# Loading and starting a recurrent kernel: biases spread by TensorE, the first x products split around the first gates, weights in halves, last outputs in pieces

## The chip, the cores and the metric

The kernel runs on one core of a Trainium2 chip. The metric is device time in microseconds for one execution, the median of several runs. TensorE (PE) multiplies into PSUM, VectorE (DVE), ScalarE (ACT) and GpSimd (POOL) do the rest, and the queues of SyncE (SP) and, after the change, of ScalarE issue the transfers, which 16 DMA engines carry out.

## The reference

A gated recurrent unit over 512 steps, batch 16, 512 channels, all in float32, with the input added to its output:

```
for each step t (H starts as cond_1024):
    Z = sigmoid(x_t Wxz' + bxz + H Whz' + bhz)
    R = sigmoid(x_t Wxr' + bxr + H Whr' + bhr)
    Ht = tanh(x_t Wxh' + bxh + (R * H) Whh' + bhh)
    H = Z * H + (1 - Z) * Ht
    out_t = x_t + H Whq' + bhq
```

## The kernel before, in words

**Layout.** A product has as its stationary operand a block of x or of the state (channels by 16 or 32 columns) and streams 64 to 192 columns of weights, so a gate's result lies in PSUM as four row groups of 32 (`j` in 0..3) by columns. VectorE turns it back (`turn_pre`, a 32x32 transpose) so that ScalarE can apply sigmoid or tanh with channels on partitions. In float32 one `nc.tensor.matmul` shows as two MATMUL and two LDWEIGHTS records in the profile.

**Turns.** The 512 steps go in 128 turns of four steps (c = 0..3), that is two pairs of steps, "pair a" in the PSUM banks `gates[0]` and "pair b" in `gates[1]`. The first turn and the last are written out; the 126 between are one hardware loop (`turn_loop`). A step runs on TensorE as `recur(R)`, `recur(Z)`, `recur(H)`, 16 matmuls each. R needs the whole state before it (`state_ready`), H needs R's gate times the state (`reset_ready`), and the new state comes from a scan on VectorE (`renew`). Between these stand parts of the next turn's x products and of the output projection, so that TensorE has work while the other engines turn and activate.

**x products by seven.** For later turns the x parts of both pairs are made with Strassen's scheme: sums of x blocks (`x_sum`, on GpSimd) times sums of weights (`w_sum`, called t1 to t4 in the rows). VectorE makes t1 and t2 before the first turn, t3 and t4 inside step 0 of the first turn. The first turn's own x parts are plain products with the two weight tiles `wx_v` (columns of Z and half of R) and `wx_u` (H and the other half of R).

**The start.** SyncE's queue issues, in this order: xr, wx_v, bias_in (384 KB: the gate biases already repeated over 128 rows), wx_u, h0, and the recurrent weights wh of R, Z, H (1 MB each). VectorE adds the two biases (`bias_rows`), ScalarE copies the sum into both pairs' PSUM banks, and only then TensorE adds the first x products (64 matmuls with wx_v for both pairs, 24 dummies called `keep_busy`, 32 matmuls with wx_u for both pairs). VectorE raises `state_ready` after t1 and t2, which need wx_u. Two groups of `keep_busy` (16 and 20 matmuls on zeros) fill step 0 between R and Z and between Z and H. The x of the second turn is loaded into the same tile xr once the first products have read it.

**The end.** In the last turn the outputs of the last pair are 16 matmuls (`project_y(1)`) that wait for all three parts of the last state, then an addition on VectorE and a store.

Of the kernel before, what the change touches and what calls it, by code (L numbers as in the profile page):

```python
# [6 lines left out]
ALU = mybir.AluOpType  # L7
# [28 lines left out]
def gru(nc, x_t, x_res, h0, w_x, w_h, w_q, b_gate, b_out, out):  # L36
# [9 lines left out]
    with ExitStack() as ctx:  # L46
# [15 lines left out]
        bias_in = sb("bias_in", [P, 2, 2, W])  # L62
# [3 lines left out]
        xr = sb("xr", [P, 2, G, Q])  # L66

# [41 lines left out]
        wh_loaded = [sem(f"wh_loaded{g}") for g in range(3)]  # L109
        wq_loaded = sem("wq_loaded")  # L110
        bias_out_loaded = sem("bias_out_loaded")
        t_ready = [sem(f"t{n}_ready") for n in range(1, 5)]
        bias_loaded = sem("bias_loaded")
        bias_ready = sem("bias_ready")
        h0_loaded = sem("h0_loaded")
        h0_ready = sem("h0_ready")
        banks_primed = sem("banks_primed")
        x_filled = sem("x_filled")
# [88 lines left out]
        def _(sp):  # L207
# [13 lines left out]
            def turn(i, reload, last):  # L221
                if not last:

                    sp.wait_ge(xr_used, i + 1)
                    sp.wait_ge(s3_ready, i)
                    load_xr(i + 1)
# [21 lines left out]
            sp.wait_ge(wh_loaded[H], 16)  # L248
# [17 lines left out]
        def _(pool):  # L266
            def sum_1(n):

                pool.wait_ge(xr_loaded, 16 * (n + 1))
# [34 lines left out]
            nc.gpsimd.memset(zeros[:], 0.0).then_inc(zeros_ready, 1)  # L304
            nc.gpsimd.memset(scanned[:], 0.0).then_inc(zeroed, 1)
# [8 lines left out]
        def _(pe):  # L314
# [61 lines left out]
            def recur(g, i, c, first=False):  # L376
# [4 lines left out]
                for m in range(G):  # L381
                    for h, (a, _) in enumerate(PARTS):
# [46 lines left out]

            def turn(i, first, last):  # L430

                recur(R, i, 0, first)
                if first:
                    keep_busy(4)
                recur(Z, i, 0, first)
                if first:
                    keep_busy(5)
# [14 lines left out]
                if not last:  # L452
                    pe.wait_ge(xr_loaded, 16 * (i + 2))
                    p1(0, WIDE)
# [9 lines left out]
                if not first:  # L464
                    pe.wait_ge(xb_loaded, 16 * i)
                    pe.wait_ge(t_ready[3], 1)
# [63 lines left out]
            for to, at in ((gates[0], Z_AT), (gates[0], 512), (gates[1], Z_AT), (gates[1], 512), (y_bank, 0), (p5_bank, 0)):  # L530
                for j in range(G):
                    nc.tensor.matmul(to[Q * j:Q * (j + 1), at:at + P], zeros[:, 0:Q], zeros[:], start=True, stop=True)
            for to, at in ((gates[0], 512), (gates[1], 512), (p5_bank, 0), (y_bank, 0), (y_bank, P), (y_bank, 2 * P)):
                for j in range(G):
                    mm = nc.tensor.matmul(to[Q * j:Q * (j + 1), at + P:at + 2 * P], zeros[:, 0:Q], zeros[:], start=False,
                                          stop=True, skip_group_check=True)
            mm.then_inc(banks_primed, 1)

            pe.wait_ge(x_filled, 2)
            pe.wait_ge(xr_loaded, 16)  # L540
            pe.wait_ge(wx_loaded[0], 16)
            for par in range(2):
                for m in range(G):
                    for cols in (WIDE, NARROW):
                        products(gates[par], Z_AT, xr[:, par], wx[0], m, cols)
            keep_busy(6)
            pe.wait_ge(wx_loaded[1], 16)
            for par in range(2):
                for m in range(G):
                    mm = products(gates[par], H_AT, xr[:, par], wx[1], m, ALL)  # L550
            mm.then_inc(xr_used, 1)
            turn_loop(pe, turn)
            for h in range(N):
                pe.wait_ge(state_ready[h], 2 * pairs + 1)
# [3 lines left out]
        def _(act):  # L558
# [58 lines left out]
            act.wait_ge(bias_ready, 1)  # L617
            act.wait_ge(banks_primed, 1)
# [219 lines left out]
```

## Time and profile before

| what | value |
|---|---|
| median of 3 runs | 2160.69 us (2160.05 to 2160.74) |
| the profiled execution | 2159.91 us, of which the span from first to last instruction is 2158.1 us |
| PE busy | 2142.6 us, 99% |
| DVE / ACT / POOL busy | 1621.6 / 844.8 / 167.3 us |
| DMA | 62.68 MB, mean 29 GB/s |
| instruction packets | 17, 0.28 MB |

PE's busy share is an average over a loop in which PE is always busy and a start and an end in which it waits. The busy time is of pipelined matmuls, whose ends are modelled.

### The profile page before, as it was taken

What the parts mean: (1) busy time and instruction counts of PE and PEld (TensorE: products, weight loads), DVE (VectorE), ACT (ScalarE), POOL (GpSimd) and SP (SyncE); (2) the same over time, 40 slices, a digit from 0 to 9 for tenths busy, and PEclk for the clock granted to TensorE, in tenths of its full rate; (3) what the DMA queues carried; (4) which work ended last, traced back from release to release, by engine and by line L of the source; (5) the groups of instructions that cost most, each with busy time, mean ns of one, the idle gap of its engine ahead of it and who ended that gap; (6) DMA issues with size and microseconds to landing.
All of it is one profiled execution on the core that took longest, in us unless ns stands there. A gap on an engine that the chain in (4) does not pass through costs nothing.

```text
span 2158.1 us, 193479 instructions
## 1 busy us (share of the span) xinstructions
PE 2142.6 (99%) x85184; PEld 2131.3 (99%) x85184; DVE 1621.6 (75%) x9469; ACT 844.8 (39%) x4864; POOL 167.3 (8%) x520
## 2 busy tenths in 40 slices
PE   7999999999999999999999999999999999999999
PEld 7999999999999999999999999999999999999998
DVE  5777777777777777777777777777777777777777
ACT  2333433343334333433343334333343334333333
POOL 1000000000000000000000000000000000000000
PEclk9999999999999999999999999999999999999999
DMA  4010001000000000000000010001000000010000
GB/s 160 26 29 24 24 26 28 24 24 26 27 26 24 25 27 26 24 24 27 28 24 24 26 29 24 24 26 29 24 24 26 29 24 24 26 29 24 24 26 27
DMA packets 111764, 62.68 MB, mean 29 GB/s; under 512 B 28800, under 2 KB 110848, under 8 KB 110976
## 3 DMA queue, kind: packets, MB, share of 16 engines
q1 hardware_dynamic: 111744, 62.37, 9.9%
q8 instruction: 17, 0.28, 0.1%
q14 instruction: 3, 0.02, 0.0%
HBM read 45.55 MB, written 16.78 MB: 29 GB/s over the span
## 4 chain that ended last, share of the span: by engine, by line
PE 99%; DVE 1%; DMA 0%; issue 0%; ACT 0%; SPq 0%
PE gates L396 61%; PE p_bank L321 16%; PE gates L321 12%; PE y_bank L329 10%; DMA bias_in<-in_b_gate 0%; DVE pre_t L628 0%; DVE scanned L692 0%; DVE t L735 0%; DVE t L749 0%; DVE reset_state L731 0%; PE p_bank L428 0%; DVE yt L683 0%; ACT scan_on L614 0%; PE y_bank L371 0%; ACT gates L620 0%
## 5 line engine op out<-in xcount | busy, mean ns | idle before, releaser
L396 PE MATMUL gates<-wh,scanned 128*16 128x128 f32 x32768 | 1047.4, 273 | 3.9 <-DVE scanned L692 2.3
L396 PEld LDWEIGHTS gates<-wh,scanned 128*16 128x16 f32 x32768 | 935.7, 104 | 5.8 <-DVE scanned L692 3.1
L628 DVE STREAM_TRANSPOSE pre_t<-gates 128x32 f32<-128x32 f32 (+2 forms) x3584 | 618.1, 216 | 209.5 <-PE gates L396 157.3
L396 PE MATMUL gates<-wh,reset_state 128*16 128x128 f32 (+1 forms) x16384 | 600.4, 273 | 1.9 <-issue 1.6
L396 PEld LDWEIGHTS gates<-wh,reset_state 128*16 128x16 f32 (+1 forms) x16384 | 471.6, 103 | 5.2 <-issue 2.6
L599 ACT ACTIVATE r_gate<-pre_t 128x16 f32<-128x16 f32 (+1 forms) x1536 | 234.6, 215 | 511.6 <-DVE pre_t L628 511.6
L321 PE MATMUL p_bank<-t,s 128*32 128x192 f32 x7112 | 361.7, 303 | 0.0
L614 ACT ACTIVATE scan_on<-pre_t 128x16 f32<-128x16 f32 (+1 forms) x1536 | 238.1, 218 | 267.0 <-DVE pre_t L628 267.0
L692 DVE TENSOR_TENSOR_SCAN scanned<-scan_by,scan_on 128x32 f32<-128x32 f32 x2048 | 300.9, 210 | 28.6
L321 PEld LDWEIGHTS p_bank<-t,s 128*32 128x32 f32 x7112 | 284.9, 110 | 2.8
L746 DVE TENSOR_TENSOR scan_on<-z_gate,scanned 128x64 f32<-128x64 f32 x512 | 116.4, 227 | 174.1 <-ACT z_gate L603 174.1
L731 DVE TENSOR_TENSOR reset_state<-r_gate,scanned 128x16 f32<-128x16 f32 (+1 forms) x1536 | 223.2, 182 | 27.4
L602 ACT ACTIVATE scan_by<-pre_t 128x64 f32<-128x64 f32 x512 | 137.4, 268 | 265.7 <-DVE pre_t L628 265.7
L321 PE MATMUL p_bank<-wx_v,xr 128*32 128x128 f32 x4064 | 197.3, 246 | 0.0
L321 PE MATMUL gates<-wx_v,xr 128*32 128x128 f32 (+1 forms) x4192 | 163.9, 248 | 5.2 <-ACT gates L620 5.2
L329 PE MATMUL y_bank<-yt,ys 128*32 128x64 f32 x6096 | 160.8, 219 | 0.0
L329 PEld LDWEIGHTS y_bank<-yt,ys 128*32 128x32 f32 x6096 | 153.1, 110 | 0.4
L321 PEld LDWEIGHTS p_bank<-wx_v,xr 128*32 128x32 f32 x4064 | 142.2, 110 | 0.0
L321 PEld LDWEIGHTS gates<-wx_v,xr 128*32 128x32 f32 x4192 | 136.0, 111 | 5.4 <-ACT gates L620 5.4
L329 PE MATMUL y_bank<-wq,scanned 128*32 128x64 f32 x4064 | 132.2, 219 | 0.0
L603 ACT ACTIVATE z_gate<-pre_t 128x64 f32<-128x64 f32 x512 | 123.0, 240 | 0.0
L321 PE MATMUL gates<-t,x_b 128*32 128x128 f32 x4064 | 121.7, 246 | 0.1
(76 smaller groups left out, 1571.7 us busy)
## 6 DMA issues: line engine op xcount, KB each, us to landing
xr<-in_x_t SPq DMA_DIRECT2D x128, 128.0 KB, 2.1
y_io<-in_x_res SPq DMA_DIRECT2D x256, 64.0 KB, 2.0
out<-y_io SPq DMA_DIRECT2D x256, 64.0 KB, 1.6
x_b<-in_x_t SPq DMA_DIRECT2D x127, 32.0 KB, 1.7
wx_v<-in_w_xv SPq DMA_DIRECT2D x1, 1536.0 KB, 6.6
wx_u<-in_w_xu SPq DMA_DIRECT2D x1, 1536.0 KB, 11.7
wh<-in_w_hr SPq DMA_DIRECT2D x1, 1024.0 KB, 13.0
wh<-in_w_hz SPq DMA_DIRECT2D x1, 1024.0 KB, 14.9
```

The costliest lines, as they stand in the source:

```text
L321: mm = nc.tensor.matmul(to[Q * j:Q * (j + 1), at + a:at + b], of[:, m, :], w[:, m, W * j + a:W * j + b], start=start, stop=stop, skip_grou ...
L329: mm = nc.tensor.matmul(y_bank[Q * j:Q * (j + 1), at:at + YW], of(m), w(m, j), start=False, stop=(m == half - 1), skip_group_check=True)
L396: mm = nc.tensor.matmul(gate_rows(g, par, slice(Q * j, Q * j + rows)), of, w, start=False, stop=(m == G - 1), skip_group_check=True)
L599: nc.scalar.activation(r_gate[:, a:b], pre_t[R][:, a:b, mine], ACT.Sigmoid).then_inc(r_ready[h], 1)
L602: nc.scalar.activation(z_not, pre_t[Z][:, :, mine], ACT.Sigmoid, scale=-1.0)
L603: nc.scalar.activation(z_gate[:], pre_t[Z][:, :, mine], ACT.Sigmoid).then_inc(z_ready, 1)
L614: nc.scalar.activation(cand[:, a:b], pre_t[H][:, a:b, mine], ACT.Tanh).then_inc(cand_ready[h], 1)
L628: nc.vector.transpose(flat(pre_t[g][:, a:b]), gate_part(g, par, a, b)).then_inc(done, 1)
L692: mm = nc.vector.tensor_tensor_scan(scanned[:, par, m, (1 + s) * B:(2 + s) * B, :].rearrange("p b k -> p (b k)"), scan_by[:, m].rearrange( ...
L731: nc.vector.tensor_tensor(reset_state[:, a:b, B:2 * B], r_gate[:, a:b], old[:, a:b], ALU.mult).then_inc(reset_ready[h], 1)
L746: nc.vector.tensor_tensor(kept, z_gate[:], old, ALU.mult)
```

## The change

- The gate biases come as 12 KB on two partitions (`bias_in`, one row for the x biases, one for the h biases). TensorE multiplies them by a tile of ones, which adds the two and spreads them over the 32 rows of each group, directly into the gate banks; ScalarE copies one result back to `bias_rows`.
- The first x has a tile of its own (`x_first`); xr's second-turn load no longer waits.
- Before the first turn only pair a's x products are made. Pair b's stand where the two groups of `keep_busy` in step 0 stood: the wx_v part between R and Z, the wx_u part between Z and H.
- H's recurrent weights come in two halves, and `recur(H)` waits for the upper one at its third block.
- ScalarE issues bias_in, x_first and h0; SyncE starts with wx_v.
- t4 is made in two halves, one in step 0, one in step 1.
- The last outputs wait for each part of the state separately.
- The banks are no longer cleared by zeros where the biases now start them, so 24 of the 48 clearing matmuls go and 16 bias matmuls come.

```
-            load_xr(0)
-            sp.dma_start(wx[0][:], w_x[0]).then_inc(wx_loaded[0], 16)
-            sp.dma_start(bias_in[:], b_gate).then_inc(bias_loaded, 16)
-            sp.dma_start(wx[1][:], w_x[1]).then_inc(wx_loaded[1], 16)
-            sp.dma_start(h0_in[:], h0).then_inc(h0_loaded, 16)
-            for g in range(3):
+            for n in range(2):
+                sp.dma_start(wx[n][:], w_x[n]).then_inc(wx_loaded[n], 16)
+            for g in (R, Z):
                 sp.dma_start(wh[g][:], w_h[g]).then_inc(wh_loaded[g], 16)
-            sp.wait_ge(xr_used, 1)
+            sp.dma_start(wh[H][:, 0:half], w_h[H][:, 0:half]).then_inc(wh_loaded[H], 16)
+            sp.dma_start(wh[H][:, half:G], w_h[H][:, half:G]).then_inc(wh_upper_loaded, 16)
             load_xr(1)
             load_xb(1)
 
-            sp.wait_ge(wh_loaded[H], 16)
+            sp.wait_ge(wh_upper_loaded, 16)
...
                 for m in range(G):
+                    for h, (a, _) in enumerate(PARTS):
+                        if m == a:
+                            pe.wait_ge(state_ready[h], 2 * pairs - 1 + 2 * par)
...
+            def first_products(par, n):
+                pe.wait_ge(wx_loaded[n], 16)
+                for m in range(G):
+                    if n == 1:
+                        products(gates[par], H_AT, x_first[:, par], wx[1], m, ALL)
+                    else:
+                        for cols in (WIDE, NARROW):
+                            products(gates[par], Z_AT, x_first[:, par], wx[0], m, cols)
...
                 recur(R, i, 0, first)
                 if first:
-                    keep_busy(4)
+                    pe.wait_ge(bias_ready, 1)
+                    first_products(1, 0)
                 recur(Z, i, 0, first)
                 if first:
-                    keep_busy(5)
+                    first_products(1, 1)
...
-            act.wait_ge(bias_ready, 1)
-            act.wait_ge(banks_primed, 1)
-            for par in range(2):
-                nc.scalar.copy(gates[par][:, Z_AT:Z_AT + 2 * W], bias_rows[:].rearrange("p a c -> p (a c)")
-                               ).then_inc(x_filled, 1)
+            act.dma_start(bias_in[:], b_gate).then_inc(bias_loaded, 16)
+            act.dma_start(x_first[:], x_t[0]).then_inc(x_first_loaded, 16)
+            act.dma_start(h0_in[:], h0).then_inc(h0_loaded, 16)
+            act.wait_ge(biases_in, 1)
+            nc.scalar.copy(bias_rows[:].rearrange("p a c -> p (a c)"), gates[1][:, Z_AT:Z_AT + 2 * W]
+                           ).then_inc(bias_ready, 1)
...
-                        nc.vector.tensor_tensor(w_sum[3][:], wx[0][:, half:G], w_sum[1][:], ALU.subtract
+                    if first and c < half:
+                        nc.vector.tensor_tensor(w_sum[3][:, c], wx[0][:, half + c], w_sum[1][:, c], ALU.subtract
                                                 ).then_inc(t_ready[3], 1)
```

TensorE around the first step's R, before the change. x<n> behind a row is the number of matmuls, wh0, wh1, wh2 are the recurrent weights of R, Z and H, and p7_bank takes the dummies:

```order
L428 MATMUL p7_bank<-zeros 32x128 x24
L321 MATMUL gates0<-wx_u,xr 32x192 [waits wu_loaded]
L321 MATMUL gates0<-wx_u,xr 32x192 x15
L321 MATMUL gates1<-wx_u,xr 32x192 x16
L396 MATMUL gates0<-wh0,scanned 16x2x64 [waits state_ready0,wh_loaded0]
...
L428 MATMUL p7_bank<-zeros 32x128 x16
L396 MATMUL gates0<-wh1,scanned 16x128 [waits wh_loaded1]
L396 MATMUL gates0<-wh1,scanned 16x128 x15
L428 MATMUL p7_bank<-zeros 32x128 x20
L396 MATMUL gates0<-wh2,reset_state 16x128 [waits reset_ready0,wh_loaded2]
```

The same place after it:

```order
L437 MATMUL p7_bank<-zeros 32x128 x24
L325 MATMUL gates0<-wx_u,x_first 32x192 [waits wu_loaded]
L325 MATMUL gates0<-wx_u,x_first 32x192 x15
L405 MATMUL gates0<-wh0,scanned 16x2x64 [waits state_ready0,wh_loaded0]
...
L325 MATMUL gates1<-wx_v,x_first 32x128 [waits wv_loaded,bias_ready]
...
L405 MATMUL gates0<-wh1,scanned 16x128 [waits wh_loaded1]
L405 MATMUL gates0<-wh1,scanned 16x128 x15
L325 MATMUL gates1<-wx_u,x_first 32x192 [waits wu_loaded]
L325 MATMUL gates1<-wx_u,x_first 32x192 x15
L405 MATMUL gates0<-wh2,reset_state 16x128 [waits reset_ready0,wh_loaded2]
```

Pair b's products (gates1) moved from ahead of R to the two places of the dummies; 16 with 192 columns stand ahead of R where 32 stood.

The start of SyncE's queue, before:

```order
L209 DMA xr<-in_x_t 128x256
L238 DMA wx_v<-in_w_xv 128x3072
L239 DMA bias_in<-in_b_gate 128x768
L240 DMA wx_u<-in_w_xu 128x3072
L241 DMA h0_in<-in_h0 128x64
L243 DMA wh0<-in_w_hr 128x2048
```

and after:

```order
L243 DMA wx_v<-in_w_xv 128x3072
L243 DMA wx_u<-in_w_xu 128x3072
L245 DMA wh0<-in_w_hr 128x2048
L245 DMA wh1<-in_w_hz 128x2048
L246 DMA wh2<-in_w_hh 128x1024
```

xr, bias_in and h0 left this queue; ScalarE's begins with bias_in 2x1536, x_first 128x256 and h0.

VectorE from the first transpose of Z on, before:

```order
L628 STREAM_TRANSPOSE pre_t1<-gates0 128x128 [waits z_pre_done]
L746 TENSOR_TENSOR scan_on<-z_gate,scanned 128x64 [waits z_ready]
L749 TENSOR_TENSOR t4<-wx_v,t2 128x1536 [waits t2_ready]
L628 STREAM_TRANSPOSE pre_t2<-gates0 128x32 [waits h_pre_done]
```

and after, with a second such t4 row behind the same two rows of step 1:

```order
L646 STREAM_TRANSPOSE pre_t1<-gates0 128x128 [waits z_pre_done]
L764 TENSOR_TENSOR scan_on<-z_gate,scanned 128x64 [waits z_ready]
L769 TENSOR_TENSOR t4<-wx_v,t2 128x768 [waits t2_ready]
L646 STREAM_TRANSPOSE pre_t2<-gates0 128x32 [waits h_pre_done]
```

Half of t4 moved from ahead of step 0's transposes of H to ahead of step 1's.

## Rows read from the trace of the kernel before

**Rows 1.** The page: span, an engine's busy time, a queue's packets, MB, share.

```profile
span 2158.1 us, 193479 instructions
PE 2142.6 (99%) x85184; PEld 2131.3 (99%) x85184; DVE 1621.6 (75%) x9469; ACT 844.8 (39%) x4864; POOL 167.3 (8%) x520
q8 instruction: 17, 0.28, 0.1%
```

**Rows 2.** Chain that ended last, first 40 us: start us, us, what.

```profile
1.66 7.07 DMA bias_in<-in_b_gate
...
10.29 4.50 PE gates L321 x128
...
16.10 2.60 PE gates L321 x64
...
18.70 0.43 PE gates L396 x14
19.13 1.18 issue
...
22.10 1.67 DVE t L735
...
24.69 1.67 DVE t L749
...
27.05 1.96 PE gates L396 x64
...
29.66 0.31 issue
...
35.81 0.22 PE y_bank L329 x16
```

**Rows 3.** DMA in the first 60 us: queue; then issues, KB, us to landing.

```profile
q8 instruction: 12, 0.20, 1.4%
...
wx_u<-in_w_xu SPq DMA_DIRECT2D x1, 1536.0 KB, 11.7
wh<-in_w_hr SPq DMA_DIRECT2D x1, 1024.0 KB, 13.0
```

**Rows 4.** Timeline of SyncE's queue: start us, us, instruction.

```profile
2.13 0.43 SPq L240 DMA_DIRECT2D wx_u<-in_w_xu  x1
...
3.39 0.44 SPq L243 DMA_DIRECT2D wh<-in_w_hr  x1
...
40.06 0.33 SPq L209 DMA_DIRECT2D xr<-in_x_t  x1
...
59.34 0.35 SPq L209 DMA_DIRECT2D xr<-in_x_t  x1
...
75.96 0.35 SPq L209 DMA_DIRECT2D xr<-in_x_t  x1
```

**Rows 5.** Timeline of VectorE, 13 to 31 us.

```profile
13.97 1.76 DVE L761 TENSOR_TENSOR t<-wx_u,wx_v 128x1536 f32<-128x1536 f32 x1 [4.66 <-DMA wx_u<-in_w_xu]
15.77 1.76 DVE L764 TENSOR_TENSOR t<-wx_u,t 128x1536 f32<-128x1536 f32 x1
21.17 0.45 DVE L628 STREAM_TRANSPOSE pre_t<-gates 128x32 f32<-128x32 f32 x3 [3.64 <-PE gates L396]
...
29.86 0.23 DVE L746 TENSOR_TENSOR scan_on<-z_gate,scanned 128x64 f32<-128x64 f32 x1 [0.47 <-ACT z_gate L603]
30.85 0.45 DVE L628 STREAM_TRANSPOSE pre_t<-gates 128x32 f32<-128x32 f32 x3 [0.76 <-PE gates L396]
```

**Rows 6.** Windows: length, PE, PEld, DVE, ACT, POOL busy (count), PE clock, DMA.

```profile
10.50:13.80 3.30, 3.30 (x92) 3.30 (x88) 0.00 (x0) 1.04 (x1) 0.00 (x0) 0.51 1.00 405
...
2157.50:2158.10 0.60, 0.00 (x0) 0.00 (x0) 0.00 (x0) 0.00 (x0) 0.00 (x0) 0.52 0.00 0
```

**Rows 7.** Timeline of the last us.

```profile
2153.40 0.58 DVE L692 TENSOR_TENSOR_SCAN scanned<-scan_by,scan_on 128x32 f32<-128x32 f32 x4
...
2154.13 1.08 PE L371 MATMUL y_bank<-wq,scanned 128*32 128x128 f32 x32 [0.42 <-DVE scanned L692]
```

More of the change, by code:

```diff
@@ L60, in gru @@
         w_sum = [sb(f"t{n}", [P, half, CW]) for n in range(1, 5)]
-        bias_in = sb("bias_in", [P, 2, 2, W])
+        bias_in = sb("bias_in", [2, G, 2 * W])
+        ones = sb("ones", [2, Q])
         bias_rows = sb("bias_rows", [P, 2, W])
@@ L66, in gru @@
         xr = sb("xr", [P, 2, G, Q])
+        x_first = sb("x_first", [P, 2, G, Q])
         x_b1 = sb("x_b1", [P, half, Q])
@@ L116, in gru @@
         h0_ready = sem("h0_ready")
-        banks_primed = sem("banks_primed")
-        x_filled = sem("x_filled")
+        ones_ready = sem("ones_ready")
+        x_first_loaded = sem("x_first_loaded")
         p5_filled = sem("p5_filled")
@@ L304, in _ @@
             nc.gpsimd.memset(zeros[:], 0.0).then_inc(zeros_ready, 1)
+            nc.gpsimd.memset(ones[:], 1.0).then_inc(ones_ready, 1)
             nc.gpsimd.memset(scanned[:], 0.0).then_inc(zeroed, 1)
@@ L381, in recur @@
                 for m in range(G):
+                    if first and c == 0 and g == H and m == half:
+                        pe.wait_ge(wh_upper_loaded, 16)
                     for h, (a, _) in enumerate(PARTS):
@@ L529, in _ @@
             pe.wait_ge(zeros_ready, 1)
-            for to, at in ((gates[0], Z_AT), (gates[0], 512), (gates[1], Z_AT), (gates[1], 512), (y_bank, 0), (p5_bank, 0)):
+            for to, at in ((y_bank, 0), (p5_bank, 0)):
                 for j in range(G):
                     nc.tensor.matmul(to[Q * j:Q * (j + 1), at:at + P], zeros[:, 0:Q], zeros[:], start=True, stop=True)
-            for to, at in ((gates[0], 512), (gates[1], 512), (p5_bank, 0), (y_bank, 0), (y_bank, P), (y_bank, 2 * P)):
+            for to, at in ((p5_bank, 0), (y_bank, 0), (y_bank, P), (y_bank, 2 * P)):
@@ L534, in _ @@
                 for j in range(G):
[L535 to L541, printed above, removed]
-            for par in range(2):
-                for m in range(G):
-                    for cols in (WIDE, NARROW):
-                        products(gates[par], Z_AT, xr[:, par], wx[0], m, cols)
@@ L546, in _ @@
-            keep_busy(6)
-            pe.wait_ge(wx_loaded[1], 16)
-            for par in range(2):
-                for m in range(G):
-                    mm = products(gates[par], H_AT, xr[:, par], wx[1], m, ALL)
-            mm.then_inc(xr_used, 1)
+                    nc.tensor.matmul(to[Q * j:Q * (j + 1), at + P:at + 2 * P], zeros[:, 0:Q], zeros[:], start=False,
+                                     stop=True, skip_group_check=True)
+            pe.wait_ge(ones_ready, 1)
+            pe.wait_ge(bias_loaded, 16)
@@ new lines, in _ @@
+            for par in range(2):
+                for at, cols in ((Z_AT, P), (512, 2 * P)):
+                    for j in range(G):
+                        mm = nc.tensor.matmul(gates[par][Q * j:Q * (j + 1), at:at + cols], ones[:],
+                                              bias_in[:, j, at - Z_AT:at - Z_AT + cols], start=True, stop=True)
+            mm.then_inc(biases_in, 1)
+            pe.wait_ge(x_first_loaded, 16)
+            first_products(0, 0)
+            keep_busy(6)
+            first_products(0, 1)
@@ L552, in _ @@
             turn_loop(pe, turn)
-            for h in range(N):
-                pe.wait_ge(state_ready[h], 2 * pairs + 1)
             project_y(1).then_inc(y_projected, 1)
@@ L755, in turn @@
                         renew(t, h, par, s)
-            dve.wait_ge(bias_loaded, 16)
-            nc.vector.tensor_tensor(bias_rows[:], bias_in[:, 0], bias_in[:, 1], ALU.add).then_inc(bias_ready, 1)
+            dve.wait_ge(bias_ready, 1)
             dve.wait_ge(wx_loaded[0], 16)
@@ L813 @@
         "h0": _np.asarray(inputs["cond_1024"]).T.reshape(P, G, batch),
-        "b_gate": _np.stack([in_rows(in_vu(*(by_block(bias(a + g)) for g in "rzh"))).reshape(P, 2, -1)
-                             for a in ("bx", "bh")], axis=1),
+        "b_gate": _np.stack([in_vu(*(by_block(bias(a + g)) for g in "rzh")) for a in ("bx", "bh")]),
         "b_out": in_rows(bias("bhq")),
```

11 lines of the change are left out of this document (6 added, 5 removed).

## The prediction

> **What bounds the kernel now.** I read the page first: the span is 2158.1 us, and TensorE is busy for 2142.6 us of it [rows 1]. The missing 15 us lie where TensorE waits, so I read the chain of waits over the first 40 us and the last ones. The loop is TensorE's own: SyncE loads xr once a turn, at 59.34 and at 75.96, 16.62 us apart [rows 4]. The loop's instructions do not change, so whatever the change brings is a shift of the whole loop by what the start gives, plus what the end gives.
>
> In the start the chain goes: bias_in, which is issued at 1.66 and takes 7.07 us; VectorE's sum and ScalarE's copies; x products from 10.29; more of them from 16.10; then R; then a gap of 1.18 us called "issue", in which TensorE waits for nothing that the profile shows; then VectorE's t3 and t4, 1.67 us each [rows 2]. The bias looks like the culprit, but it is not alone: wx_u lands only at 2.13 + 11.7 = 13.83 us [rows 3, 4], and VectorE's t1 and t2, which stand ahead of `state_ready`, run from 13.97 to 15.77 + 1.76 = 17.53 [rows 5]. R could therefore not begin before 17.5 even without the bias. It begins about 18.5. This second chain is what is left when the bias is gone, and the sum goes along it.
>
> **The gap.** The trace holds 17 packets of instructions, 0.28 MB, 12 of them in the first 60 us [rows 1, 3]. The program has 472 + 332 + 288 = 1092 matmuls for TensorE, which makes 64 matmuls for a packet. Ahead of the gap stand 48 + 64 + 24 + 32 + 7 = 175 (R's first 14 records are 7 matmuls [rows 2]); the gap of 0.31 us at 29.66 comes near 303, which is 2 x 64 further. I take the gaps for TensorE waiting for its next block of instructions. The first pass through the loop says the same: from the load at 40.06 to that at 59.34 are 19.28 us, 2.66 more than 16.62 [rows 4], and it is the pass in which the loop's code is new. The Trainium skill (Runtime: NRT & Kernel Launch, "Instruction fetch mechanics") describes such 16 KiB blocks and calls the cost of crossing one mostly hidden. By that sentence this kernel would lose nothing there, and the gap's term below would be zero. The trace does not agree in its start, with 1.18 us.
>
> **The change, part by part.**
>
> *Landing of wx_u.* 1024 KB of wh R land at 3.39 + 13.0 = 16.39, 2.56 us after wx_u [rows 3, 4], so 384 KB of biases were worth 0.96 us and 12 KB are 0.03. wx_v is first in its queue now, one issue (0.43 us) earlier, but x_first's 128 KB (0.32 us) run beside it. So wx_u lands 0.93 to 1.36 us earlier; I take 1.1, since the stream was full from its start. Below that, 0.6 if the engine that ends last is slow for another reason. VectorE then ends t1 and t2 at 16.43, and R starts at 16.5. wh R, 1.1 earlier too, is there at 15.3. h0 is on the other queue and early.
>
> *TensorE up to there.* The bias matmuls (16, on two rows) and pair a's wx_v part must be over before wx_u lands at 12.7. A record with 128 columns costs (1.96 - 0.27) / 64 = 26.4 ns, one with 64 columns 0.22 / 16 = 13.8 ns [rows 2], so pair a's 64 records are 1.3 us, 2.6 at half clock; wx_v is there soon after 7. Its 32 records of wx_u (2.60 / 64 = 41 ns each [rows 2]) take 1.3 and end at 14.0. Both are covered; so are ScalarE's issues and its copy to `bias_rows`, by the wait for wx_u.
>
> *R without the gap.* R's 32 records take 0.85 us and the last needs 0.27 to end, so the transposes of R, which began at 21.17 [rows 5], begin at 17.6: 3.6 us earlier. This needs the gap gone. Matmul 175 is now the last of Z (112 ahead of R, 16, 32, 15). The block that it opens was asked for, if one block ahead, at matmul 111: before at the first dummies near 14.8, and it was there at 20.31, 5.5 us later. Now 111 is the last product ahead of R, at 14.0, so the block is there at 19.5; TensorE gets to it at 17.35 + 1.3 + 0.85 = 19.5. I charge 0.1. Bounds: 0, and 1.2 if the transfer is slower behind the weights.
>
> *Pair b's products and t4.* After R, TensorE has 1.3 (wx_v part), 0.85 (Z), 1.3 (wx_u part), 0.85 + 0.27 (H): H is done at 21.9. VectorE had its transposes of H free at 26.36, 5.19 after the transposes of R [rows 2, 5]; half of t4 (0.83) leaves, so it is free at 17.6 + 4.36 = 22.0. They tie. Pair b's parts cost nothing, because t3 and t4 on VectorE cover them, and half of t4 is a gain of 0.83; a cover of 0.1 us is all there is. H's upper half of weights, before the last of the stream, is there near 20, and its third block needs it at 21.2.
>
> *Step 1.* It starts at 27.05 - 3.57 - 0.83 = 22.65. The other half of t4 (0.83) now stands behind the row at 29.86 + 0.23, ending 3.87 us into the step; H's transposes began 3.80 into it [rows 5]. Cost 0.1; if the gap of 0.31 there is gone too, the step could have been that much shorter and is not.
>
> *To the end of the loop's first pass.* 44 matmuls fewer are read before it, but the pass is held to the pace of its blocks in both kernels. Their edges move against the code, and a wait of some 0.3 us may come or go. I take 0, with 0.6 to either side. wq, now asked for some 1.3 us earlier, is needed only in step 2. xr for the second turn loads behind the weights, unwaited for.
>
> *The end.* `project_y(1)` starts at 2154.13, after all four scans (2153.40, 0.58 us) [rows 7]. Its first block can start after the first scan, some 0.25 us in, at 2153.68, and its third not before 2154.0; 16 records each half, 0.44 us, fit. Gain 0.45, at least 0.2. The waits put into `project_y(0)` are long satisfied.
>
> **Sum:** 3.57 - 0.1 + 0.83 - 0.1 + 0 + 0.45 = 4.65 us off the profiled 2159.91 us (span 2158.1 and 1.8 around it). The median is 0.8 above that execution; the same shift gives 2160.69 - 4.7 = 2156.0 us. A measurement of this kernel can tell about 0.2% from no change, 4.3 us, so the sum is just beyond that bound.
>
> **Rivals.**
>
> 1. *The clock.* TensorE idles now from about 10.1 (end of the dummies) to 12.7, and from 14.0 to 16.5. Before, its clock was 0.51 of full between 10.5 and 13.8, after five idle microseconds, and it is 0.52 again at 2157.5, 2.3 us after the last matmul ended [rows 6, 7]. So a gap of 2.5 us may be enough. At half rate the 5 us from R to H have next to no cover, and 3.4 us of it cost 1.7. If the fall comes earlier it costs nothing, as TensorE waits then. Taking 1.1 as its middle: 2157.1, at worst 2157.7. Against it: the clock stayed whole over the 1.18 us gap.
> 2. *The start does not move as much.* The engine that delivers wx_u last is held up by something other than bytes, or the block of instructions is late behind wh and the gap only moves to Z. Either loses about 1 us: 2157.0.
> 3. *More.* wx_u may land with the pack rather than behind a late engine; then t1, R and all behind it gain another microsecond: 2155.0.
> 4. *The loop refetches (slower).* The loop's 332 matmuls are 5.2 blocks. It began 472 - 175 = 4.64 blocks behind the gap's edge, 0.64 into a block, and touched six. After, it begins 3.95 behind it, and 0.95 + 5.2 touches seven, with one more read ahead. If TensorE keeps only seven, it refetches every turn, and each turn costs what the first pass did: 126 x 2.66 = 335 us more, 2491 us. It decides between seven and eight blocks. For it speaks that the trace shows no more than seven kept; against it only that nothing says seven is the end. The Trainium skill's same section gives TensorE's instruction memory 128 KiB, eight such blocks, by which it just fits; it also warns that a taken branch beyond two blocks fetches again, and there the trace disagrees, with 12 packets for the first 60 us and five for all the rest.
>
> **How the numbers follow.** Forecast as summed: 0.58. Clock: 0.2. Start moves less: 0.14. More: 0.05. Refetch: 0.03. The forecast's own range, 2155.3 to 2156.8, has about three quarters beyond the bound of 2156.4; the clock and the smaller start almost nothing. Faster 0.5, the same 0.46, slower 0.04. The range over the cases is 2154.9 to 2157.7.
>
> **What would show it.** In the profile after: wx_u's landing at 12.7; t2's end at 16.4; R's transposes at 17.6; no "issue" before R is through; step 1 at 22.7; loads of xr at 35.8 and 55.0; `project_y(1)` 0.45 us nearer to the scans. The clock of 10 to 22 us decides rival 1. A load of xr every 16.6 us rules out rival 4, more instruction packets than 17 would speak for it. The prediction is wrong if R starts later than 17.2, if PE and not VectorE holds H by more than 0.5 us, or if the first pass through the loop is not 19.3 us long.

## The result and the profile after

The changed kernel takes 2172.03 us (median, 2170.14 to 2172.45) against 2160.55 us for the kernel before in the same comparison: ratio 1.0051, 95% interval 1.0041 to 1.0061. It is slower by 11.5 us, where 4.7 us off were forecast. The profiled spans, 2168.4 against 2158.1 us, differ by 10.3. The profiled execution of the changed kernel is one of the two faster ones of its six (2170.15 us), so what follows splits 10.3 us and not the whole 11.5.

The page of the changed kernel, for [rows 1]:

```profile
span 2168.4 us, 193180 instructions
PE 2150.5 (99%) x85096; PEld 2133.2 (98%) x85096; DVE 1624.4 (75%) x9469; ACT 845.4 (39%) x4863; POOL 169.2 (8%) x521
q8 instruction: 16, 0.26, 0.0%
```

88 matmul records fewer, and TensorE is busy 7.9 us longer. The start does not do that: in the first 59.34 us TensorE is busy for 46.01 us, where before it was 48.19. SyncE's queue after the change, for [rows 4], with the last load of xr too:

```profile
39.81 0.33 SPq L214 DMA_DIRECT2D xr<-in_x_t  x1
60.38 0.35 SPq L214 DMA_DIRECT2D xr<-in_x_t  x1
76.99 0.35 SPq L214 DMA_DIRECT2D xr<-in_x_t  x1
93.75 0.35 SPq L214 DMA_DIRECT2D xr<-in_x_t  x1
...
2131.63 0.35 SPq L214 DMA_DIRECT2D xr<-in_x_t  x1
```

and of the kernel before, the load behind those of [rows 4] and the last:

```profile
92.59 0.35 SPq L209 DMA_DIRECT2D xr<-in_x_t  x1
...
2121.24 0.35 SPq L209 DMA_DIRECT2D xr<-in_x_t  x1
```

This splits the 10.3 us. There is one load a turn, and 123 turns between the load at 75.96 (after: 76.99) and the last. Up to there: +1.0. The 123 turns: 2121.24 - 75.96 = 2045.28 us before, 16.628 each; 2131.63 - 76.99 = 2054.64 after, 16.704 each; +9.4. The last load to the end of the span: 36.9 before, 36.8 after. So the loop, in which the change touches no matmul (some waits differ, and TensorE has one register instruction fewer in it), runs 0.076 us a turn longer, and its turns are no longer alike (first 16.61, 16.76 and 16.63, later most of 16.69 and some of 16.73, where before each took 16.63).

The start, in the chain of waits of the changed kernel, for [rows 2]:

```profile
1.31 8.97 DMA x_first<-in_x_t
...
10.33 2.79 PE gates L325 x64
13.12 1.94 PE p_bank L437 x48
...
16.36 0.30 issue
16.66 0.32 PE gates L325
...
20.03 2.03 issue
...
25.45 1.72 PE gates L405 x52
27.18 0.96 issue
...
29.82 0.87 DVE t L769
...
46.89 1.25 issue
```

bias_in is gone from the chain, but another small load stands in its place: x_first, 128 KB, on ScalarE's queue beside the weights on SyncE's, lands at 10.3. Wherever TensorE has to wait without a releaser, the gaps are larger than before, not smaller: 2.03 and 0.96 where 1.18 and 0.31 stood. VectorE there, for [rows 5]:

```profile
11.62 1.76 DVE L780 TENSOR_TENSOR t<-wx_u,wx_v 128x1536 f32<-128x1536 f32 x1 [11.62 <-DMA wx_u<-in_w_xu]
13.42 1.76 DVE L783 TENSOR_TENSOR t<-wx_u,t 128x1536 f32<-128x1536 f32 x1
18.05 0.45 DVE L646 STREAM_TRANSPOSE pre_t<-gates 128x32 f32<-128x32 f32 x3 [2.88 <-PE gates L405]
...
30.61 0.44 DVE L646 STREAM_TRANSPOSE pre_t<-gates 128x32 f32<-128x32 f32 x3
```

t1 and t2 end at 15.2, 2.3 us before their old end and 1.2 before the forecast. VectorE is ready for R, and TensorE is late.

The end, for [rows 7]:

```profile
2161.84 2.79 SPq L220 DMA_DIRECT2D y_io<-in_x_res  x2
...
2163.58 1.08 PE L378 MATMUL y_bank<-wq,scanned 128*32 128x128 f32 x32
2164.54 0.29 DVE L650 TENSOR_TENSOR y_io<-p_bank,y_io 128x128 f32<-128x128 f32 x1 [0.65 <-DMA y_io<-in_x_res]
2164.86 1.89 SPq L224 DMA_DIRECT2D out<-y_io  x2
2166.08 0.29 DVE L650 TENSOR_TENSOR y_io<-y_bank,y_io 128x128 f32<-128x128 f32 x1 [1.25 <-DMA y_io<-in_x_res]
```

The last matmuls come nearer to the scans, as forecast (0.28 us behind their start, before 0.73), and then both additions wait for the loads of y_io. Before, the last addition waited for TensorE:

```profile
2155.27 0.29 DVE L632 TENSOR_TENSOR y_io<-y_bank,y_io 128x128 f32<-128x128 f32 x1 [0.86 <-PE y_bank L371]
```

### The profile page after: what moved, and what is told of

Same layout as the page of the kernel before. It is cut to its first block, busy times and chain, and to the rows that moved or that the text cites. A ratio compares the mean times of both kernels' runs of the same rounds, so it can differ in the third digit from the quotient of the medians.

```text
span 2168.4 us, 193180 instructions
## 1 busy us (share of the span) xinstructions
PE 2150.5 (99%) x85096; PEld 2133.2 (98%) x85096; DVE 1624.4 (75%) x9469; ACT 845.4 (39%) x4863; POOL 169.2 (8%) x521
## 4 chain that ended last, share of the span: by engine, by line
PE 98%; DMA 1%; DVE 0%; issue 0%; ACT 0%; ACTq 0%; SPq 0%; DVEq 0%
PE gates L405 61%; PE p_bank L325 15%; PE gates L325 12%; PE y_bank L333 10%; DMA x_first<-in_x_t 0%; DMA out<-y_io 0%; PE p_bank L437 0%; DVE pre_t L646 0%; DMA y_io<-in_x_res 0%; DVE scanned L710 0%; DVE yt L701 0%; ACT scan_on L631 0%; DVE t L769 0%; DVE y_io L650 0%; DVE reset_state L749 0%
## 5 line engine op out<-in xcount | busy, mean ns | idle before, releaser
L405 PE MATMUL gates<-wh,scanned 128*16 128x128 f32 x32768 | 1052.2, 273 | 5.9 <-issue 3.7
L405 PEld LDWEIGHTS gates<-wh,scanned 128*16 128x16 f32 x32768 | 934.3, 104 | 13.8 <-issue 4.7
L405 PE MATMUL gates<-wh,reset_state 128*16 128x128 f32 (+1 forms) x16384 | 598.0, 273 | 1.6 <-issue 1.2
L405 PEld LDWEIGHTS gates<-wh,reset_state 128*16 128x16 f32 (+1 forms) x16384 | 464.1, 103 | 2.6 <-issue 1.5
L333 PE MATMUL y_bank<-yt,ys 128*32 128x64 f32 x6096 | 167.5, 219 | 0.4 <-issue 0.4
L333 PEld LDWEIGHTS y_bank<-yt,ys 128*32 128x32 f32 x6096 | 158.6, 110 | 2.1 <-issue 0.6
L325 PE MATMUL gates<-wx_v,xr 128*32 128x128 f32 x4064 | 155.7, 246 | 0.0
L325 PEld LDWEIGHTS gates<-wx_v,xr 128*32 128x32 f32 x4064 | 128.0, 110 | 0.0
## 6 DMA issues: line engine op xcount, KB each, us to landing
wx_u<-in_w_xu SPq DMA_DIRECT2D x1, 1536.0 KB, 10.3
wh<-in_w_hr SPq DMA_DIRECT2D x1, 1024.0 KB, 12.4
```

What stands on the lines that cost most here:

```text
L325: mm = nc.tensor.matmul(to[Q * j:Q * (j + 1), at + a:at + b], of[:, m, :], w[:, m, W * j + a:W * j + b], start=start, stop=stop, skip_grou ...
L333: mm = nc.tensor.matmul(y_bank[Q * j:Q * (j + 1), at:at + YW], of(m), w(m, j), start=False, stop=(m == half - 1), skip_group_check=True)
L405: mm = nc.tensor.matmul(gate_rows(g, par, slice(Q * j, Q * j + rows)), of, w, start=False, stop=(m == G - 1), skip_group_check=True)
```

## The experiments

**The theories.** TensorE's instructions come in blocks of 256, 64 matmuls of four instructions; the gaps of the start stand at the borders between two blocks, which I call edges. The target of the loop's branch is the loop's first instruction, to which every turn jumps back. The change has 173 instructions fewer ahead of the loop. Before, the first edge inside the loop lay some 92 instructions behind the loop's first one. Now it lies at 92 + 173 - 256 = 9. The difference of 173 is counted in the programs; the 92 is reckoned back from where the gaps of the start stand, and edges so placed lie about one matmul behind the gaps, so all distances here may be some five instructions too large, the same for all kernels. Theory A: an edge right behind the target of the loop's branch makes every turn longer. Theory B: the changed waits inside the loop (t4's count of 2, xr's counts) do it. For the start, theory C: the late x_first delays pair a's products, and with them the moment at which the block for matmul 175 is asked for. Dummies ahead of the loop move the edge by 16 instructions a group and change nothing inside it.

### Padding the changed kernel, and the kernel before

```
             mm.then_inc(biases_in, 1)
+            keep_busy(11)
```

The other two have `keep_busy(1)` at the same place, and, in the kernel before, `keep_busy(5)` behind `mm.then_inc(banks_primed, 1)`.

> The changed kernel with 11 more groups of dummy matmuls (44 matmuls, 176 instructions) behind the bias matmuls, where TensorE idles from 5.4 to 10.3 us. Counted in matmuls, the loop then starts again where it started before the change, some 22 matmuls ahead of an edge between two blocks of instructions; in the changed kernel it starts about 9 instructions ahead of one. Theory A (the turn of the loop is longer because of where its code lies against the blocks): turns of 16.63 us again, some 9 us faster than the changed kernel, about 2163 us. Theory B (the changed waits, or one register instruction fewer in the loop, make the turn longer): turns of 16.69 or more stay, 2172 us.

> The changed kernel with 1 more group of dummies (4 matmuls, 16 instructions): the loop starts some 7 instructions behind an edge instead of 9 ahead of it. Theory A in its narrow form (what costs is an edge right behind the branch's target): 16.63 us turns, about 2163 us. If instead it is the number of blocks that the loop touches, or which edges fall where TensorE has little queued, turns lie between 16.63 and 16.74. Theory B: as the changed kernel, 2172 us.

> The kernel before with 5 groups of dummies (20 matmuls, 80 instructions) in TensorE's idle time from 5.1 to 10.3 us. Nothing of the change is in it, but the loop then starts some 12 instructions ahead of an edge. Theory A: turns of 16.69 to 16.74, about 2169 us, slower by 0.4%. Theory B: 2160.6 us, the same.

The changed kernel with 11 groups, SyncE's queue:

```profile
38.10 0.33 SPq L214 DMA_DIRECT2D xr<-in_x_t  x1
57.55 0.35 SPq L214 DMA_DIRECT2D xr<-in_x_t  x1
74.16 0.35 SPq L214 DMA_DIRECT2D xr<-in_x_t  x1
...
2119.44 0.35 SPq L214 DMA_DIRECT2D xr<-in_x_t  x1
```

2119.44 - 74.16 is 2045.28 us again: adding 44 matmuls of zeros took the whole 9.4 us of the loop away. It did more than that: the span of 2155.8 is 12.6 us below the changed kernel's, 2.8 of them in the start (load of xr at 74.16 for 76.99) and 0.4 at the end, and so the time is far below the 2163 us that was expected. The ratio to the kernel before is 0.9989 [0.9980, 0.9999]. With one group (edge 7 instructions ahead of the target) it is 2045.28 us too, span 2158.0, ratio 0.9992 [0.9982, 1.0002]; there the start gives 0.2 us (load of xr at 76.82) and the end 0.9. The kernel before with five groups (edge 12 behind) is slower, as the changed kernel is, though by less than expected: ratio 1.0023 [1.0013, 1.0033], and its 123 turns, with xr loads at 76.59 and 2125.99, take 2049.40 us, 16.662 each, of 16.63, 16.68 and 16.72 by turns; 16.69 to 16.74 were expected. Theory A holds in both directions. Theory B is refuted: the changed waits run at 16.628, and the old ones can be made to lose.

### x_first on SyncE's queue

```
+            sp.dma_start(x_first[:], x_t[0]).then_inc(x_first_loaded, 16)
             for n in range(2):
...
-            act.dma_start(x_first[:], x_t[0]).then_inc(x_first_loaded, 16)
```

> The changed kernel with x_first issued by SyncE ahead of wx_v instead of by ScalarE; the code of TensorE is the same. Its landing took 9.0 us on ScalarE's queue beside the weights; ahead of them it should land near 3, as xr did. Theory C (x_first behind the weights holds the start): pair a's products begin near 7.6 instead of 10.3, R begins at 15.3 instead of 16.8, the block behind matmul 111 is asked for earlier and the gap of 2.0 us in Z goes or shrinks; 2 to 4 us faster, 2168 to 2170 us. Rival: wx_u lands later by x_first's bytes and the gap stays: under 1 us. The turns stay at 16.69 to 16.74 in either.

2171.17 us, ratio 1.0051 [1.0034, 1.0067]. The chain names a weight load now, and the gap is still there:

```profile
2.60 15.15 DMA wh<-in_w_hz
...
18.86 2.72 issue
```

The gap ends at 21.58 instead of 22.06, so only 0.5 us are won at it; by the load of xr (75.34 for 76.99) it is 1.65 us. The loop is no better, (2133.03 - 75.34) / 123 = 16.729 a turn, and loses 3.0 us more than the changed kernel's. That its code and its edge are the same and its turns are not is open; the turns of both are of 16.69 or of 16.73 us, and here nearly all are of the longer kind. So the late x_first costs something, but it is not what makes the gap. Three windows of this kernel, the first in the gap (the last number but two is the granted clock):

```profile
20.00:22.00 2.00, 0.43 (x13) 0.42 (x16) 0.00 (x0) 0.00 (x0) 0.00 (x0) 1.00 0.06 14
22.00:24.00 2.00, 2.00 (x47) 1.98 (x42) 1.41 (x3) 0.40 (x2) 1.02 (x1) 0.68 0.73 168
24.00:26.00 2.00, 1.83 (x31) 1.33 (x23) 0.50 (x4) 0.30 (x3) 0.41 (x2) 0.50 0.96 391
```

TensorE waited most of 20 to 22 us and then had its lower level of 1.2 GHz (0.5) for some 3.4 us. From the gap's end to step 1 it needed 4.65 us (21.57 to 26.22), where the changed kernel, at full clock, needed 3.39 (22.06 to 25.45). The kernel with one group has the same behind its gap (0.56 and 0.59 from 22 to 26). In the changed kernel itself the clock is whole from 14.3 on, so its time is not explained by this.

### Where the edge lies, and one matmul group less or more in the loop

The third kernel leaves out `keep_busy(6)` between pair a's two parts; the second has 15 groups of padding.

> The changed kernel with 15 groups of dummies after the bias matmuls: the block edge comes to some 25 instructions (6 matmuls) behind the loop's first, where the changed kernel has 9, and the padded ones 89 (no loss) and 7 ahead of it (no loss). Theory A with a reach of a few dozen instructions: turns longer than 16.628, by 0.02 to 0.08 us, 2 to 10 us in all. Rival 1: only an edge within some ten instructions costs anything, turns of 16.628. Rival 2: it is the end of the loop's body that matters (54 instructions behind an edge in the changed kernel); here it lies 70 behind one, as in the kernel with one group, which lost nothing: turns of 16.628.

> The changed kernel without the 24 dummies between pair a's two parts: 96 instructions fewer ahead of the loop, so the edge lies some 105 behind its first instruction. Theory A: turns of 16.628 us, the whole 9.4 us of the loop come back with fewer instructions, not more, and the span is about 2168.4 - 9.4 - 1 = 2158 or less. The gap in the start moves from the end of Z to H's recurrence (matmul 175), whose block is asked for behind R at about 17.9 and is there near 22, where VectorE's t3 covers part of it: step 1 starts at 24 to 25 instead of 25.45, and the span is 2154.5 to 2156.5. Rival (any change against the kernel before but padding costs the loop, or the changed waits do): turns of 16.7. Rival on the clock: TensorE, without dummies, runs at half clock beyond R, and step 1 starts later than 25.45.

With 15 groups (edge 25 behind the target) the loads at 76.44 and 2121.72 give 2045.28 us: no loss, which refutes the reach of a few dozen that I had written down, and rival 1 holds. (The body's end lies 38 instructions behind an edge there, and not 70 as the expectation says; rival 2 is tested below.) Without the 24 dummies (edge 105 behind) it is 2045.28 again (74.20 to 2119.48), span 2155.8, ratio 0.9988 [0.9978, 0.9997]. This is the answer to whether padding does something of its own: the loop's loss goes with fewer instructions ahead as well, and the start is 2.8 us shorter here too.

In all of these the end of the loop's body moves with its start. To part them, one group of dummies is put into the loop's turn:

```
                     pe.wait_ge(s3_ready, i)
+                    keep_busy(1)
                     p7(0, ALL)
```

> The changed kernel with one group of dummies (4 matmuls, 16 instructions) added inside the loop's turn, ahead of p7. The edge stays 9 instructions behind the loop's first; the end of the body moves from 54 to 70 instructions behind an edge, where the kernel with one group ahead of the loop lost nothing. The four matmuls themselves add about 8 x 26.4 ns = 0.21 us a turn. Theory A (the edge behind the branch's target): turns that vary and are 0.04 to 0.1 us longer than those of the next kernel. Rival (the edge that counts is the one ahead of the branch itself): turns all of one length, 16.84.

> The same with 11 groups of dummies ahead of the loop as well: the edge lies 89 instructions behind the loop's first, the body ends 150 behind one. The base of the comparison under both theories: turns of one length, about 16.628 + 0.21 = 16.84 us.

> The same with 15 groups ahead of the loop: the edge lies 25 behind the loop's first, which cost nothing before, and the body ends 54 behind an edge, as in the changed kernel. Theory A: 16.84 us a turn, as with 11 groups. Rival (the body's end decides): longer by 0.04 to 0.1, and varying.

SyncE's queue with nothing ahead of the loop, edge 9 behind the target:

```profile
77.06 0.35 SPq L214 DMA_DIRECT2D xr<-in_x_t  x1
...
2162.49 0.35 SPq L214 DMA_DIRECT2D xr<-in_x_t  x1
```

and with 15 groups ahead, the body's end at the old unlucky place:

```profile
75.93 0.35 SPq L214 DMA_DIRECT2D xr<-in_x_t  x1
...
2148.07 0.35 SPq L214 DMA_DIRECT2D xr<-in_x_t  x1
```

(2162.49 - 77.06) / 123 = 16.955 against (2148.07 - 75.93) / 123 = 16.847; with 11 groups 16.847 too. The spans are 2200.1, 2184.9 and 2184.9 us. The longer turns are all alike, 16.95 or 16.96, and do not vary as expected. So it is the edge behind the branch's target, not the one ahead of the branch. These three kernels and the one with 15 groups were run once each; what is compared are their 123 turns, and in all kernels without a loss these agree to 0.01 us in 2045.28. All kernels in one table, distances in instructions as said under the theories, turns from the loads of xr:

| kernel | first edge, from the target | us a turn | loss in 123 turns |
|---|---|---|---|
| one group | -7 | 16.628 | 0 |
| changed kernel | +9 | 16.704 | 9.4 |
| changed, x_first on SyncE | +9 | 16.729 | 12.4 |
| one more group in the body | +9 | 16.955 (base 16.847) | 13.3 |
| before, five groups | +12 | 16.662 | 4.1 |
| 15 groups; the same and one in the body | +25 | 16.628; 16.847 | 0 |
| 11 groups; the same and one in the body | +89 | 16.628; 16.847 | 0 |
| 11 groups with the mends of the next section (three kernels) | +89 | 16.628 | 0 |
| before | +92 | 16.628 | 0 |
| without the 24 dummies | +105 | 16.628 | 0 |

The trace also shows where in the turn the time goes. TensorE's weight loads at the head of a turn of the changed kernel (L405 are R's):

```profile
1045.33 0.10 PEld L405 LDWEIGHTS gates<-wh,scanned 128*16 128x16 f32 x1
1045.34 0.11 PEld L333 LDWEIGHTS y_bank<-wq,scanned 128*32 128x32 f32 x1
1045.49 0.49 PEld L405 LDWEIGHTS gates<-wh,scanned 128*16 128x16 f32 x20
```

and of the kernel with 11 groups:

```profile
1038.37 0.11 PEld L333 LDWEIGHTS y_bank<-wq,scanned 128*32 128x32 f32 x1
1038.41 0.58 PEld L405 LDWEIGHTS gates<-wh,scanned 128*16 128x16 f32 x19
```

Averaged over 115 turns and counted from the turn's first weight load, the second matmul's load comes 0.158 us later in the changed kernel than in the one with 11 groups; from the fourth matmul to the end of the turn everything is late by about the same 0.07. With x_first on SyncE it is 0.185, and 0.10 from then on; with a group in the body, against its base, 0.188 and 0.105. So the whole loss arises at the turn's head, where the edge lies. In the kernel before with five groups it cannot be placed so cleanly. No block is moved again for it: in none of these kernels does the instruction queue move anything between 77 and 2130 us. Seven kernels have one more transfer of code at 75 to 76 us, three of them without a loss (one group; 15 groups, alone and with a group in the body), so it is not that either. Why an edge there costs time stays open.

### The end, and all mends together

```
+            for par in range(2):
+                sp.dma_start(flat(x_first[:, par]), x_res[pairs - 2 + par]).then_inc(last_loaded[par], 16)
             turn(turns - 1, reload=True, last=True)
             for par in range(2):
-                sp.wait_ge(stored[par], 16 * (turns - 1))
-                load_res(pairs - 2 + par, par)
...
```

The last additions and stores use that tile, and the kernel has the 11 groups too. The next kernel has x_first on SyncE's queue as well as 11 groups, and the last one all three.

> The changed kernel with 11 groups of dummies, and the last pair's residuals loaded before the last turn into the tile of x_first, which is free by then, added and stored from there, so that the last additions wait for no late load. If the end's gain of 0.45 us was given back to that load, the second addition comes some 1.0 us behind the start of the last 16 matmuls instead of 1.95, and the span is about 0.9 us shorter than the padded kernel's, 2154.9; VectorE's row shows TensorE as what ends its wait. Rival: the store alone sets the end, and the span stays within 0.3 of 2155.8. Turns stay at 16.628.

> The changed kernel with 11 groups of dummies after the bias matmuls and x_first issued by SyncE ahead of wx_v. Theory A (where the loop lies against the instruction blocks): the edge is some 89 instructions behind the loop's first, so every turn takes 16.628 us although x_first moved. Theory C (the late x_first holds pair a's products, and with them the block edge ahead of R): without padding the move brought the third load of xr 1.65 us nearer and the step at the gap 0.5 nearer; here I expect 0.5 to 1.6 us off the padded kernel's span of 2155.8, so 2154.2 to 2155.3. Rival: with 44 more matmuls to be read, the blocks alone set the start, and the span stays at 2155.8 within 0.3.

> The changed kernel with 11 groups of dummies after the bias matmuls, x_first issued by SyncE ahead of wx_v, and the last pair's residuals in the tile of x_first. From the three measured apart: turns of 16.628; the start of the padded kernel with x_first on SyncE (third load of xr at 73.25 against 75.96 before the change, 2.7 us less); the end 1.0 us shorter than the kernel before's (4.0 us behind the start of the last matmuls, here 3.5, and these 0.45 nearer). Span 2158.1 - 2.7 - 0.9 = 2154.5, and the ratio about 0.9983. Rival: x_first's landing, 9 to 11 us on ScalarE's queue, is as uneven on SyncE's, and the start gives back up to 1 us: 2155.5.

The end of the kernel with the tile of its own, VectorE and TensorE:

```profile
2152.52 1.08 PE L379 MATMUL y_bank<-wq,scanned 128*32 128x128 f32 x32
2152.74 0.27 DVE L656 TENSOR_TENSOR x_first<-p_bank,x_first 128x128 f32<-128x128 f32 x1
...
2153.67 0.29 DVE L656 TENSOR_TENSOR x_first<-y_bank,x_first 128x128 f32<-128x128 f32 x1 [0.66 <-PE y_bank L379]
```

The second addition comes 1.15 us behind the start of the last matmuls instead of 2.50 in the changed kernel, and TensorE ends its wait. From the last load of xr to the end of the span are 35.6 us (2156.0 - 2120.38), with padding alone 36.4 (2155.8 - 2119.44), in the changed kernel 36.8, before 36.9. So the load held the end. What that is worth is less sure than the 1.2 us against before: with the changed kernel's own end this stretch takes between 35.9 (one group) and 36.8 us, as the load lands early or late, and with the tile of its own 35.6 both times. The ratios with and without it, 0.9987 and 0.9989, do not tell the two apart. The span as a whole came out at 2156.0, not 2154.9, because the start was 0.9 us later in this execution (load of xr at 75.10 for 74.16), in which x_first took 10.93 us to land. Ratio 0.9987 [0.9977, 0.9996].

With x_first on SyncE and padding: span 2155.1, 0.7 less than padded alone, within what was expected, but the ratio does not show it, 0.9992 [0.9982, 1.0001] against 0.9989. All three: 2157.25 us against 2160.43, ratio 0.9985 [0.9976, 0.9994], span 2155.5 where 2154.5 was expected. Its x_first lands 2.3 us after its issue at 0.75, so the rival (an uneven landing) is not what took the microsecond: the end has its 35.6, and the loop's first pass, between the loads of xr at 38.05 and 57.98, takes 19.9 us where the kernel with x_first on SyncE and padding took 18.8 (37.80 to 56.64).

### What paces the start

The chain of the kernel with 11 groups, which has no late edge in its loop:

```profile
16.64 2.05 issue
...
26.70 1.28 issue
...
42.42 0.41 issue
...
49.73 0.76 issue
...
53.99 0.32 issue
```

They stand at matmuls 174, 302, 556, 682 and 746 of this program, 42 to 46 more than multiples of 64 (the few other instructions make the drift), and where the other kernels have such gaps, at the same numbers within one.

That they are waits for code is shown by the transfers of the instruction queue (q8 on the page), which the trace keeps one by one: 16 KB each, 0.9 to 1.6 us long. In the changed kernel the second begins at 19.73 and takes 0.96 us, and the gap at matmul 175 ends at 22.06, 1.4 us behind it; the third begins at 25.84, and the next gap ends at 28.14, 1.3 us behind its end. The first 62 us of the 14 kernels hold 76 gaps of over 0.2 us called "issue", and every one ends 1.2 to 1.6 us behind the end of such a transfer.

How fast new code comes on the average can be read from the gap at 175 to the end of the loop's first pass, where SyncE loads xr for the second time in these rows (60.38 in the changed kernel), in the kernels that have that gap:

| kernel | gap ends | load of xr | blocks | us a block |
|---|---|---|---|---|
| before | 20.31 | 59.34 | 9.83 | 3.97 |
| changed | 22.06 | 60.38 | 9.14 | 4.19 |
| one group | 21.83 | 60.21 | 9.20 | 4.17 |
| 11 groups | 18.69 | 57.55 | 9.83 | 3.95 |
| 15 groups | 17.78 | 59.76 | 10.08 | 4.16 |
| x_first on SyncE | 21.58 | 58.72 | 9.14 | 4.06 |
| without the 24 dummies | 21.78 | 57.59 | 8.77 | 4.08 |

(Blocks: matmuls ahead of the loop, plus the loop's 332, minus 175, over 64.) It is 3.95 to 4.19 us in all of them, though waits, clock and weights differ; a turn of the running loop needs 16.628 / 5.19 = 3.20 a block. It is an average and not one duration: from one edge to the next it is 6.1 us in the changed kernel (matmul 175 to 239, 22.07 to 28.15) and 3.2 in the one with 11 groups (matmul 431 to 493, 36.01 to 39.18). Nor does the number of blocks alone set the time. The 11 groups put 44 matmuls back, 0.69 of a block, which at 4 us a block would be 2.75 us; the stretch from the gap's end to the load grew by 0.5 (38.86 for 38.32). So the gaps are waits for code, but how much of the start the code as a whole sets is not shown.

The block of matmul 175 comes 5.1 to 6.1 us after matmul 111 began in the kernels of the table and the one with a group in the body, but for one: in the changed kernel 111 is among the last products ahead of R, begun at 16.66 behind a gap of its own of 0.30, and the gap at 175 ends at 22.06. With 11 groups, pair a's wx_v part holds matmul 111, begun at 12.6, and the gap ends at 18.69. The exception is x_first on SyncE, where 111 begins at 13.96 and the gap ends 7.6 us later, at 21.58 (6.3 us after matmul 112, which had to wait until 15.31). So passing the edge 2.7 us earlier won 0.5 us there, and passing it 4.1 us earlier won 3.4 with 11 groups; why they differ is open.

## Why the prediction was wrong, by its steps

**"The loop's instructions do not change, so whatever the change brings is a shift of the whole loop".** This is the step that failed, and it made +9.4 us of the 10.3. Where the loop lies against its blocks is part of the change. Without it the span would still be 0.9 us longer, not 4.7 shorter: the start's terms failed too, by 5.2 us (load of xr 1.0 later, where 4.2 earlier were forecast), and the end's by 0.4. Rival 4 named the place of the loop and even had the numbers, "0.64 into a block" before and 0.95 after, but asked only how many blocks the loop touches. That is not what counts: the kernel with 15 groups begins 25 instructions ahead of an edge, touches seven as the changed one does, and loses nothing. No block is fetched again every turn, since 16 packets serve the whole execution and none of them lies between 77 and 2150 us; the price is 0.076 us a turn and not 2.66. The cost comes from 0.95 itself, the edge some nine instructions behind the target.

**Landing of wx_u.** Right direction, better than forecast: 1.19 + 10.3 = 11.5 for 12.7, t2's end at 15.2 for 16.4.

**"Both are covered" (TensorE up to there).** Wrong. It took wx_v as the last thing that pair a's products wait for, and let x_first's 128 KB "run beside it". x_first landed at 10.3, the products ran at half clock from 10.33 and, with the 24 dummies, took until about 16.7; R's transposes are at 18.05 instead of 17.6.

**"I charge 0.1" for the gap.** It measured 2.03. The rule, that the block is asked for one block ahead and comes about 5.5 us later, fits the changed kernel (16.66 + 5.4 = 22.06) and most others, but not the one with x_first on SyncE, with 7.6. The step took matmul 111 to be passed at 14.0, and it was passed at 16.66. That is most of step 1's delay, 25.45 for 22.65. The bound of 1.2 us was too narrow as well, since it left out that pair a's products could be late.

**Pair b's products and half of t4.** They cost next to nothing by VectorE, as said: it waited 0.29 us for H. But the gain of 0.83 did not come out. The gap at matmul 175 lies between, and from R's transposes to step 1 it took 7.40 us (18.05 to 25.45) where before it took 5.88 (21.17 to 27.05). "The other half: 0.1" was too small too: it is in the chain at 29.82 with 0.87, and H's transposes begin at 30.61, 5.16 us into the step, of which 0.96 is a gap, against 3.80 before; some 0.4 is left for t4, or 0.7 if the gap of 0.31 that the step had before is taken off as well.

**The loop's first pass, "I take 0, with 0.6 to either side".** It took 20.57 us against 19.28, +1.3, outside its bound. The pass is 18.8 to 20.9 us long over these kernels; the changed one is near the upper end for a reason that I could not settle. This is one of the signs that the prediction had named for being wrong. Whether the 44 matmuls fewer to read count cannot be said: with 11 groups they are put back, and the load of xr comes 2.8 us earlier, not later.

**The end, 0.45.** TensorE's part came as forecast, from the scans at once to the last matmuls. It was given back to the load of y_io, which the step did not look at: before, it was early enough, and the last addition waited for TensorE. About 0.1 was left.

**Rival 1, the clock.** It did not come in the changed kernel. It came in three of its variants, behind gaps of 1.5 to 2.7 us, where the chip granted half for some 3.4 us. With x_first on SyncE it made the way from the gap to step 1 1.3 us longer, near the 1.1 to 1.7 that were named for it. The length of the gap does not decide it: gaps of 2.03 and 2.05 us left the clock whole.

## What to carry to other kernels

A change ahead of a loop on TensorE also moves the loop against its instruction blocks of 256. Read the period of the loop before and after; if it has grown, or turns stop being alike, count the instructions ahead of the loop and move its first instruction by some 16, up or down, before judging the change itself: here that turned a ratio of 1.0051 into 0.9992 (one group) and 0.9989 (11, where 2.8 us of the gain are the start's).

In a start of new code, look at the block edges before the waits. A gain on another engine's chain is worth nothing where the next block comes later: here t2 ended 2.3 us earlier and step 1 began only 1.6 earlier. Dummies in idle time that let TensorE pass the edge one block ahead earlier (11 groups), and leaving dummies out (the 24), each brought the loop 2.8 us forward; by how much such a move pays was not to be forecast from these runs.

When a wait is shortened at the end, ask what the next one is; here it was two 64 KB loads, each issued only after a store had landed.

## What was unexpected of the hardware

- A block edge some 9 or 12 instructions behind a loop branch's target costs 0.03 to 0.11 us every turn on the average, in most cases with turns of uneven length; at 7 ahead, and at 25, 89, 92 and 105 behind, every turn takes the same 16.628 us. The loss arises at the turn's second matmul. The Trainium skill (Runtime: NRT & Kernel Launch, "Instruction fetch mechanics") warns of taken branches whose target lies outside a window of two blocks. By that rule all these loops would fetch again every turn; the trace does not agree, with 16 or 17 packets for a whole execution in each.
- New code came at 3.95 to 4.19 us for 64 float32 matmuls on the average, which run in 3.20, and TensorE went on 1.2 to 1.6 us behind the end of a block's transfer at each of 76 gaps.
- 128 KB issued by ScalarE at 1.31, beside 1.5 MB pieces on SyncE's queue, took 8.97 us to land, and 10.93 in another run; issued first on SyncE's queue they took 2.3.
